# A scatter that adds shared chunks, and a main loop of 440 groups in place of 469

## The reference

```python
h = jnp.maximum(_layernorm(x, axis=-1), 0.0)
edge_in = jnp.concatenate([h[row], h[col], dist], axis=1)
e = jax.nn.silu(edge_in @ eW1 + eb1)
e = jax.nn.silu(e @ eW2 + eb2)
agg = jax.ops.segment_sum(e, row, num_segments=h.shape[0])
node_in = jnp.concatenate([h, agg], axis=1)
out = jax.nn.silu(node_in @ nW1 + nb1) @ nW2 + nb2
x = x + out
```

## Time and profile before

| | us |
|---|---|
| median of 3 runs (4422.91 to 4426.76) | 4424.15 |
| the profiled execution, its own time | 4420.21 |
| its span in the profile | 4418.4 |
| PE busy, of the span | 3262.5 (74%) |
| DVE busy | 2306.3 (52%) |
| ACT busy | 1932.7 (44%) |
| POOL busy | 2323.6 (53%) |

### The profile page before, as it was taken

One profiled execution on the slowest core, in us unless ns is written; L12 is line 12 of the kernel. 1 busy time (PEld: TensorE's weight loads), 2 busy tenths in 40 slices (PEclk: granted clock), 3 DMA queues, 4 the chain that ended last, 5 costly groups with the idle time before them and its releaser, 6 DMA issues.

```text
span 4418.4 us, 90846 instructions
## 1 busy us (share of the span) xinstructions
PE 3262.5 (74%) x26059; PEld 2894.1 (66%) x26060; DVE 2306.3 (52%) x7968; ACT 1932.7 (44%) x4269; POOL 2323.6 (53%) x2362
## 2 busy tenths in 40 slices
PE   5788888888767677767777777767776777776768
PEld 4476777766656666666666666666666666666664
DVE  8678787787634444444444444444444444444441
ACT  0578788787733333333333333333333333333331
POOL 0145444454555555555555555555555555555540
PEclk9788788798688998999999999998999998999999
DMA  2000000000011111111111111111111111111794
GB/s 67 10 15 19 15 20 15 21 14 19 11 43 41 41 41 41 42 41 41 41 41 42 41 41 41 41 42 41 41 41 41 42 41 41 41 41 42 40 40 83
DMA packets 379595, 161.56 MB, mean 37 GB/s; under 512 B 324822, under 2 KB 347670, under 8 KB 379478
## 3 DMA queue, kind: packets, MB, share of 16 engines
q0 software_dynamic: 75008, 126.93, 13.6%
q1 hardware_dynamic: 304310, 32.32, 5.8%
q10 hardware_dynamic: 160, 0.85, 0.1%
HBM read 139.38 MB, written 20.53 MB: 36 GB/s over the span
## 4 chain that ended last, share of the span: by engine, by line
PE 45%; another core or an unknown queue 33%; ACT 9%; DVE 8%; issue 4%; SPq 1%; DMA 0%; POOL 0%; DVEq 0%; ACTq 0%; POOLq 0%
PE bk L892 11%; PE bk L882 7%; ACT ED L1058 7%; PE bk L811 6%; PE bk L880 6%; PE bk L890 4%; PE bk L797 2%; PE bk L799 2%; PE bk L798 1%; PE bk L843 1%; DVE GA L512 1%; DVE BIG L541 1%; DVE P L446 1%; PE bk L793 1%
## 5 line engine op out<-in xcount | busy, mean ns | idle before, releaser
L372 POOL DMA_INDIRECT GA<-q_d,RB x1876 | 1821.1, 971 | 1265.1 <-remote 550.1
L699 DVE TENSOR_TENSOR BIG<-bk,BIG 128x128 f32 x1876 | 545.9, 291 | 1672.5 <-remote 1003.3
L1058 ACT ACTIVATE ED<-bk,eb1c 128x512 f32<-128x512 f32 x469 | 322.2, 687 | 1691.5 <-remote 1230.1
L880 PE MATMUL bk<-identf,GA 128*128 128x128 f32 x3752 | 903.2, 326 | 4.7 <-DVE GA L689 3.7
L359 POOL DMA_INDIRECT rec_d<-BIG,GA x468 | 493.9, 1055 | 703.7 <-ACT BIG L993 376.2
L890 PE MATMUL bk<-B,ones 128*128 128x512 bf16 x469 | 194.6, 415 | 871.8 <-ACT ED L1058 867.7
L882 PE MATMUL bk<-OHS,P 128*128 128x128 bf16 x5628 | 685.1, 236 | 0.0
L890 PEld LDWEIGHTS bk<-B,ones 128*128 128x128 bf16 x469 | 45.4, 97 | 956.5 <-ACT ED L1058 704.5
L880 PEld LDWEIGHTS bk<-identf,GA 128*128 128x128 f32 x3752 | 660.3, 220 | 5.5 <-issue 5.0
L892 PEld LDWEIGHTS bk<-W,ED 128*128 128x128 f32 x3752 | 568.5, 217 | 16.1
L892 PE MATMUL bk<-W,ED 128*128 128x128 f32 x3752 | 571.8, 303 | 0.0
(11 more groups left out here) (182 smaller groups left out, 3180.5 us busy)
## 6 DMA issues: line engine op xcount, KB each, us to landing
GA<-q_d,RB POOLq DMA_INDIRECT x1876
RB<-rec_d SPq DMA_DIRECT2D x469, 8.0 KB
rec_d<-BIG,GA POOLq DMA_INDIRECT x468
q_d<-QS SPq DMA_DIRECT2D x14, 448.0 KB
rec_d<-ED SPq DMA_DIRECT2D x16, 236.0 KB, 10.6
hT_d<-HT SPq DMA_DIRECT2D x14, 224.0 KB
P<-hT_d SPq DMA_DIRECT2D x8, 384.0 KB, 9.8
P<-in_x SPq DMA_DIRECT2D x8, 384.0 KB, 8.6
```

The source lines that it names most:

```text
L372: e.indirect_dma_start(G[k * U + u], None, q_d, bass.IndirectOffsetOnAxis(ap=RB[k][:, u, 1:2], axis=0))\
L699: e.tensor_tensor(AGG[:, ds(v, P)], banks[6 + k % 2][:, u * P:(u + 1) * P], AGG[:, ds(v, P)], ALU.add).then_inc(s["ad"], 1)
L880: e.matmul(z, G[k * U + u], identf[:, :], start=True, stop=False)
L1058: e.activation(E1[k % 2], banks[2 + k % 2][:, :], ACT.Silu, bias=eb1c[:, :]).then_inc(s["e1"], 1)
```

## The change

Neighbouring superchunks now share chunks. A bin's records go on where the last superchunk stopped, in the middle of a chunk, so a chunk of 4 records may get its records from two superchunks. For that

- the record table starts as zeros, and the scatters add into it (`compute_op=ALU.add`); a record's integers become fp32 numbers, and the position is stored plus one, so that 0 means empty (`iob` is raised by one ahead of the main loop);
- POOL waits, ahead of the first scatter of a superchunk, until all scatters of the superchunk before it have landed;
- `CHB` goes from 9 to 10 (a bin can start and end in a part of a chunk), so there are 520 scatters in place of 468, `REC`'s tables go from 36 to 40 columns, and the unused chunks of all superchunks go to one place;
- the prefix sums ahead of the loop of stage 1 are over records, not chunks, and ten small DVE instructions follow them;
- `NG` is 440, computed from the edges and the worst padding of a block to 128;
- the index of the gather is fp32 in `RB` now, so a new DVE instruction for each group, `index(g+2)`, turns it to integers (`IX`), and the gather waits for that (`s["ix"]`) in place of the record load.

```diff
-CHB = (SC * P + NBIN * (R - 1)) // (R * P) + 1
+CHB = (SC * P + 2 * NBIN * (R - 1)) // (R * P) + 1
-NG = 469
+NG = (E + NB * (P - 1)) // (P * U) + 1
...
             for q in range(NS):
                 e.wait_ge(s["rec"], q + 1)
+                if q:
+                    e.wait_ge(s[f"scat{(q - 1) % 4}"], 16 * CHB * ((q - 1) // 4 + 1))
                 for c in range(CHB):
-                    ge(e, s["a1"], min(NR, 8 * q + 10 + c) if c else 0)
+                    ge(e, s["a1"], min(NR, 8 * q + 10 + 8 * c // CHB) if c else 0)
                     e.indirect_dma_start(rec_d, bass.IndirectOffsetOnAxis(ap=IDX[q % 4][:, c:c + 1], axis=0),
-                                         REC[q % 4][:, c * R * 4:(c + 1) * R * 4], None)\
+                                         REC[q % 4][:, c * R * 4:(c + 1) * R * 4], None, compute_op=ALU.add)\
                      .then_inc(s[f"scat{q % 4}"], 16)
...
                     if u == 0:
                         ge(e, s["z1"], g - 3)
-                        e.wait_ge(s_rec[k], i * 16 + 16)
+                        e.wait_ge(s["ix"], g + 1)
                         e.sem_inc(s["gt"], 1)
                     e.indirect_dma_start(G[k * U + u], None, q_d,
-                                         bass.IndirectOffsetOnAxis(ap=RB[k][:, u, 1:2], axis=0))\
+                                         bass.IndirectOffsetOnAxis(ap=IX[k][:, u:u + 1], axis=0))\
                      .then_inc(s_g[k * U + u], 16)
...
+            link(e.tensor_scalar(iob[:, :], iob[:, :], 1.0, None, ALU.add))
...
+            def index(g, k, n):
+
+                e.wait_ge(s_rec[k], n * 16 + 16)
+                e.tensor_copy(IX[k][:, :], RB[k][:, :, 1]).then_inc(s["ix"], 1)
...
-            with e.Fori(1, NG // 4 - 1) as i:
+            last = (NG - 2) // 4
+            with e.Fori(1, last) as i:
                 for k in range(4):
+                    index(i * 4 + (k + 2), (k + 2) % 4, i + (k + 2) // 4)
                     build(i * 4 + (k + 1), (k + 1) % 4, i + (k + 1) // 4)
                     weigh(i, k)
                     add(i * 4 + (k - 2), k % 4)
```

More of the change, by code:

```diff
@@ L42, in gnn @@
     ds = bass.ds
-    rec_d = nc.dram_tensor("rec_d", (TRASH + NS * CH, R * 4), i32).ap()
+    IR = (NT + CH * R // P + 15) // 16
+    rec_d = nc.dram_tensor("rec_d", (16 * IR * P // R, R * 4), fp32).ap()
     rows_d = rec_d[0:TRASH, :].rearrange("c (r w) -> (c r) w", w=4)
@@ L106, in gnn @@
         OREC = o1
-        REC = [part(o1 + k * CW * 4, CW * 4).bitcast(i32) for k in range(4)]
+        REC = [part(o1 + k * CW * 4, CW * 4) for k in range(4)]
         o1 += 16 * CW
@@ L176, in gnn @@
         RS = [sb(f"RS{j}", [P, HF], fp32) for j in range(2)]
-        RB = [sb(f"RB{k}", [P, U, 4], i32) for k in range(4)]
+        RB = [sb(f"RB{k}", [P, U, 4], fp32) for k in range(4)]
+        IX = [sb(f"IX{k}", [P, U], i32) for k in range(4)]
         G = [GA[:, k * HF:(k + 1) * HF] for k in range(4 * U)]
@@ L188, in gnn @@
         IOJ = ED[:, 0:CH]
-        IR = (NT + 15) // 16
-        INI = ED[:, 3072:3072 + IR * 4].bitcast(i32)
-        DCI = ED[:, CH:CH + NS * CHB].rearrange("p (s m) -> p s m", m=CHB)
+        INI = ED[:, 3072:3072 + IR * 4]
+        DCI = ED[:, CH:CH + CHB]
         IOT = ED[:, 3584:3584 + NG]
-        o1 = CH + NS * CHB
+        o1 = CH + CHB
         MM = ED[:, o1:o1 + CH // 2].bitcast(bf16)
@@ L203, in gnn @@
                  "xm sq h t1 ht pq p1 r1 p2c p3 qc fin htd qd ini scat0 scat1 scat2 scat3 "
-                 "gt oh st ad tp z1 z2 ap oT of e1 e2 zero var rt hd fz fu fo fd outs one").split()
+                 "gt ix oh st ad tp z1 z2 ap oT of e1 e2 zero var rt hd fz fu fo fd outs one").split()
         s = {n: sem("s_" + n) for n in names}
@@ L344, in _ @@
             e.memset(onef[:, :], 1.0).then_inc(s["io"], 1)
[L346 to L350, removed]
+            e.memset(INI, 0.0).then_inc(s["ini"], 1)
+            for t, pat, b0, cm in ((SI[:, :], [[0, NS]], TRASH, 0), (DCI, [[P, CHB]], TRASH // 2, 1),
                                    (IOT, [[1, NG]], 0, 0), (IOJ, [[1, CH]], 0, 0)):
@@ L457, in _ @@
             e.wait_ge(s["hc"], NS)
[L458 to L461, removed]
+            link(e.tensor_copy(ccT[:, :], banks[2][:, 0:NS]))
             link(e.memset(gA[0][:, 0:1], 0.0))
@@ L471, in _ @@
             link(e.tensor_tensor(cl[:, 3:4], gs[:, NS - 1:NS], ccT[:, NS - 1:NS], ALU.add))
-            link(e.tensor_scalar(cli[:, :], cl[:, 3:4], float(CPT - 1), None, ALU.add))
-            link(e.tensor_single_scalar(cli[:, :], cli[:, :], 7 - LR, op=ALU.arith_shift_right))
+            link(e.tensor_scalar(cli[:, :], cl[:, 3:4], float(P - 1), None, ALU.add))
+            link(e.tensor_single_scalar(cli[:, :], cli[:, :], 7, op=ALU.arith_shift_right))
             link(e.tensor_scalar(cl[:, 4:5], cli[:, :], cl[:, 1:2], None, ALU.mult))
             e.sem_inc(s["tl"], 1)
+            link(e.tensor_copy(nI[:, :], gs[:, :]))
+            link(e.tensor_single_scalar(lbn[:, :].bitcast(i32), nI[:, :], R - 1, op=ALU.bitwise_and))
+            link(e.tensor_copy(dd[:, :], lbn[:, :].bitcast(i32)))
+            link(e.tensor_single_scalar(nI[:, :], nI[:, :], LR, op=ALU.arith_shift_right))
+            link(e.tensor_copy(gs[:, :], nI[:, :]))
+            link(e.tensor_tensor(ccT[:, :], ccT[:, :], dd[:, :], ALU.add))
+            link(e.tensor_scalar(nI[:, :], ccT[:, :], float(R - 1), None, ALU.add))
+            link(e.tensor_single_scalar(nI[:, :], nI[:, :], LR, op=ALU.arith_shift_right))
+            link(e.tensor_copy(ccT[:, :], nI[:, :]))
+            e.sem_inc(s["cc"], 1)
             e.wait_ge(s["lb"], 1)
             link(e.tensor_copy(lbT[:, :], banks[3][:, 0:NS]))
-            link(e.tensor_scalar(lbR[:, :], lbT[:, :], float(R), None, ALU.mult))
+            link(e.scalar_tensor_tensor(out=lbR[:, :], in0=lbT[:, :], scalar=float(R), in1=dd[:, :],
+                                        op0=ALU.mult, op1=ALU.add))
             link(e.tensor_scalar(lbn[:, :], lbT[:, :], -1.0, 0.5, ALU.mult, ALU.add))
@@ L700, in add @@
                                     AGG[:, ds(v, P)], ALU.add).then_inc(s["ad"], 1)
+            index(0, 0, 0)
+            index(1, 1, 0)
             build(0, 0, 0)
             for k in range(4):
+                index(k + 2, (k + 2) % 4, (k + 2) // 4)
                 build(k + 1, (k + 1) % 4, (k + 1) // 4)
@@ L712, in _ @@
                     add(i * 4 + (k - 2), k % 4)
-            for g in range(4 * (NG // 4 - 1), NG):
+            for g in range(4 * last, NG):
+                if g + 2 < NG:
+                    index(g + 2, (g + 2) % 4, (g + 2) // 4)
                 if g + 1 < NG:
```

21 lines of the change are left out of this document (11 added, 10 removed).

## The result

The changed kernel takes 4718.2 us in the median of 4 runs (4708.21 to 4725.58), against 4423.53 for the kernel before beside it: a ratio of 1.0665 (95% interval 1.0651 to 1.068), slower. The forecast was 4618, with a range of 4240 to 4790; the measured time lies above the 4560 to 4700 of the likeliest case. Direction and mechanism hold under the condition in which this was measured; two terms were too small. In other sessions the kernel before took 3651 to 3663 us (medians), with the same code, and there the mechanism isn't present at all.

What follows compares the result with a forecast made beforehand. The prediction took a ring of POOL's gather batches and PE's delayed signals to bound the main loop. 4420 + 164 + 15 + 5 + 8 + 2 = 4614, plus 4 for the median, gave 4618 us, range 4240 to 4790.

Steps and rivals of the forecast that it cites:

- the loop as a ring: Main loop: PE's signals come only after POOL's batch of gathers ends, making 6.57 us a group.
- The ring's law: Main loop: the period is 0.78 to start, the batch (4.86), and 0.93 to PE's next signals, 6.57 us.
- rival C: Main loop: POOL sets the pace, four gathers of 1.25, 5.0 us a group, total 3578 us; chance 0.07.
- (1): Main loop: 469 groups become 440, worth -190 us at an unchanged 6.57 us a group.
- (2): Main loop: batches wait for the CAST behind the add, pairing up at 7.37 us a group; +164 us instead of -190.
- PE runs as in the earlier trace: 4.0: Main loop: while POOL is idle before a run, PE does the next group's matmuls in 4.0 us.
- The step that I had called the thinnest: Main loop: `ap`, due 1.6 us into a batch, is not held, so a second batch follows back to back.
- rival B: Main loop: every batch holds the group that meets it, 8.99 us a group, total 5330 us; chance 0.08.
- a long run holds PE: Main loop: a run of seven or eight gathers holds PE until 1.59 us after the run's end.
- (3): Stage 1: wider tables lengthen DVE's and PE's steps, +15 us, between 0 and 30.
- (4): Stage 1: ten scatters at plain price fit; extra scatters and landing +5, PE held +8, prefix instructions +2 us.
- rival E: Stage 1: accumulating scatters cost up to twice 1.06 us, adding up to 240 us to any case; chance 0.15.

Runs made afterwards that it cites:

- experiment 1: Changed kernel with the CAST one group earlier and ahead of the add: 4336.19 us, ratio 0.9796 to the kernel before, held condition.
- experiment 2: Kernel before with only the CAST behind the add and the gathers waiting for it: 4864.67 us, ratio 1.0975, held condition.
- experiment 6: Changed kernel, code unchanged, run in the free condition: 3681.24 us beside 3651.15 for the kernel before, one run each.
- experiment 4: Changed kernel, odd superchunks adding into a second, unread table, each waiting only for the one two before: 4638.42 us, one run, held condition.
- experiment 9: Changed kernel with the early CAST and two record tables that DVE adds together: 3580.0 us, ratio 0.9781 to the kernel before, free condition.
- experiment 3: Changed kernel with plain scatters in place of accumulating ones, so shared chunks lose records: 4813.41 us, one run, held condition.

## Why the prediction was right, and where it was off

**The reading of the loop as a ring** (first part) holds in the condition that it was read from as far as this: the moment at which a batch is released sets the period, and moving one CAST makes 7.44 out of 6.58 (experiments 1 and 2, in both directions). The ring's law with a batch of another length wasn't shown. As a statement on the kernel the reading was too wide. In the free condition the same instructions run at 5.12 us, near four gathers of 1.26, and PE's signals come at once. That is the pace of rival C, to which I gave 0.07; it describes the other condition and not this one. The Trainium skill (SBUF, State Buffer, who interferes with whom) has TensorE wait for no other engine's or DMA's access to SBUF; the free condition agrees (5.12, 4.06 and 4.00 us for four, three and two gathers), and in the held one PE's signals come late all the same.

The forecast was read from a trace of the held condition and met a result from the same one. In the free condition the same change cost 0.8% (experiment 6, one run each) and not 4.4%. Nothing in the forecast saw that there are two conditions; that its trace and its result came from the same one is luck.

**(1) and (2), the count and the new wait.** Each piece of the sum came out: the CAST at 0.16 to 0.17 (0.2 said), 0.78 to the batch, gaps of 4.2 to 4.8, cycles of eight gathers 14.5 to 14.8 us apart. What failed is "PE runs as in the earlier trace rows: 4.0": where the clock has fallen in the hold a group takes 5.3, and in about 4 of 10 runs (97 of 260) `ap` is too late for a second batch. The step that I had called the thinnest, that `ap` gets through 1.6 us into a batch, holds but was needed in a part of the cycles only: in 67 of the 163 runs of eight an update of `ap` is recorded within 1.8 us of the run's start. In the other 96 it came before the run. In the double cycle of 2528.26 both `add`s of the pair are released before or at the batch's start, because the hold had also delayed `silu2` (3.27 us of idle time ahead of it at 2525.28) and with it the `mD` before, so that its `ap` came only 2.9 us after the last and not 5. So the forecast 7.37 became 7.44, a mixture with a part of rival B in it, and +164 became +195. That a long run holds PE "for all of it" was too strong: in 98 of the 163 runs of eight a `silu1` starts inside the run, over 3 us after its start, so `z1` gets through. It is `ap` that waits for the end: in these runs it passes when due in the first 1.8 us (the 67), and every one that is due 4 us in or later comes after the run. So `silu1` does not alternate between 4 and 11 us as I said it would. One slip changes nothing: a batch is 4.86 us by my own rows and stands as 4.7 in two places, which puts rival B at 9.15 and not 8.99.

**(3), widths.** With the landing wait gone (experiment 4), stage 1 with all its wider tables ends 10 us before that of the kernel before, which is within what two traces of the same stage 1 differ by (experiment 2). Since the scatters' coupling changed at the same time, the +15 isn't measured by itself; in the changed kernel POOL is the bound and the widths lie beside it.

**(4), scatters.** This is the step that was wrong, and it is rival E in part: its signs (L359 well above 1.06, stage 1 over 50 us longer) both came, and I had given it 0.15. I took an accumulating scatter at the plain 1.06 and the landing wait as hidden "behind POOL's other waits". It takes 1.63, 0.57 more, between the bounds of 1.06 and 2.12. Ten of them with nine gaps are 19.0 us, and with the wait of 2.24 the superchunk is 21.2 of POOL alone (21.47 measured), above the 19.6 that the other engines need. From there on every wait on POOL is on the path: all terms of stage 1 together were +30 and measured +93.7, and it is the +5 that was too small. In the held condition the price alone would have been harmless (experiment 4); the price and the wait together were not. In the free condition it isn't harmless: stage 1 of the kernel before takes 18.2 to 18.6 us a superchunk there, that of experiment 9, without the wait but with the dearer scatters and the wider tables, 19.3, and its first gather is 47 to 69 us later. The wait can't simply be left out: the Trainium skill (DMA: Bandwidth & Descriptors, its table of rules) asks for it between accumulating DMAs on the same bytes, and only a second table made it unnecessary.

## What to carry to other kernels

A new small instruction belongs where its inputs are ready, not where its line reads well: behind a wait for the slowest signal, 0.16 us cost 376 us in the held condition, though next to nothing in the free one. Before taking a wait as hidden, add up the engine it stands on with the new prices; POOL was at 13.6 of 19.6 us by the old ones and over the edge by the new. And where a period rests on a delay that no record explains, measure the kernel before in a second session: here it was 4424 or 3660 us, and the change cost 6.7% in the one and 0.8% in the other (one run each there).

## What was not expected of the hardware

- **Two conditions for one program.** The kernel before took 4418 to 4444 us in two sessions and 3644 to 3675 us in four later ones, constant within a session, and chip number 5 was met in both. In the first condition, PE's signals in the kernel before come only after a run of POOL's indirect DMAs has ended (0.93 us after four, 1.59 after seven in the earlier trace rows); in the second they are updated 0.01 us after the matmuls. In the changed kernel some signals get through inside a run of eight: `silu1` went on at 2519.47, 0.62 after the fourth gather's end, and at 2536.87, with the last gather still to come, and only `ap` waited for the end. What sets the condition, and by what path the signals are delayed, stays open.
- **Plain scatters in a burst delayed PE's signals in the held condition, accumulating ones did not** (experiments 3 and 4, one run each): with 10 plain ones of 1.01 us a superchunk took 23.2 us, with 10 accumulating ones of 1.63 and no pause 19.45. Whether it is the kind of the DMA or the longer time that POOL gives to each is open.
- An accumulating indirect scatter of 128 chunks of 64 bytes held POOL for 1.63 us, a plain one for 1.06.
